# Next quad's input in the first projection's bank, a fourth token buffer, later pack loads and a new order of steps in a conv, attention and Fourier block

## What is computed

```python
for L in (0, 1):                               # conv block
    rw = sigmoid(mean(x, tokens) @ Wr + br)    # router: four weights per image
    h  = relu(bn(x @ mix(rw, Wpw) + rw @ bpw)) # first projection, 24 -> 96
    h  = relu(bn(depthwise3x3(h, mix(rw, Wdw))))
    x  = x + bn(h @ mix(rw, Wpwl) + rw @ bpwl) # second projection, 96 -> 24
t = x.reshape(32, 3136, 24)
y = ln(t); q, k, v = split(y @ Wqkv + bqkv)    # 6 heads of 4
t = t + heads(q @ k.T * 4**-0.5 @ v) @ Wff + bff
t = t + qlinear(relu(qlinear(ln(t), W1, b1)), W2, b2)   # rounded to 5/2-bit float
h = fft(relu(bn(ln(t) @ w1.T)), axis=tokens)
t = t + bn(real(ifft(relu(mixed(h)))) @ w2.T)
t = t + qlinear(relu(qlinear(ln(t), W1, b1)), W2, b2)
```

## Time and profile before

| | us |
|---|---|
| median of 3 runs | 2447.91 |
| lowest and highest | 2443.51, 2450.33 |
| the profiled execution's own time | 2448.76 |
| its span, first to last instruction | 2447.0 |
| PE, DVE, ACT busy | 2087.6, 1924.6, 1583.8 |

### The profile page before, as it was taken

How to read it: one execution, slowest core, us unless ns; L and a number is a source line. 1 busy time by engine, 2 the same in 40 slices (tenths; PEclk the granted TensorE clock), 3 DMA queues, 4 the chain that set the end, 5 groups by cost and what they waited for, 6 DMA issues and landing times.

```text
span 2447.0 us, 48861 instructions
## 1 busy us (share of the span) xinstructions
PE 2087.6 (85%) x19720; PEld 1234.5 (50%) x19720; DVE 1924.6 (79%) x3745; ACT 1583.8 (65%) x2704; POOL 114.6 (5%) x290
## 2 busy tenths in 40 slices
PE   3777988999979989999789987898889998887865
PEld 2233433664446634665347634376347644663753
DVE  4986988799949999699959996698978999366253
ACT  3344447775777677765777666776767667767544
POOL 0000000000000000000000000000000000000000
PEclk9887989999979999999989997899999999987765
DMA  5001000100020000100020002000010000000000
GB/s 147 1 1 21 1 1 5 18 2 1 1 40 2 2 1 15 28 2 1 1 40 2 2 1 41 1 2 1 1 32 2 2 1 1 22 2 1 21 1 20
DMA packets 108591, 29.62 MB, mean 12 GB/s; under 512 B 104144, under 2 KB 104272, under 8 KB 107984
## 3 DMA queue, kind: packets, MB, share of 16 engines
q1 hardware_dynamic: 108368, 26.50, 5.3%
HBM read 16.85 MB, written 9.63 MB: 11 GB/s over the span
## 4 chain that ended last, share of the span: by engine, by line
DVE 40%; PE 36%; ACT 13%; issue 7%; SPq 3%; DMA 1%; ACTq 0%; DVEq 0%
DVE acc L1505 19%; PE P L757 7%; PE P L738 5%; PE P L972 4%; DVE SQ L1670 3%; PE P L1064 3%; SPq L598 3%; DVE arena L1654 3%; PE P L909 2%; DVE arena L1670 2%; PE P L779 2%; DVE roots L1670 2%; PE P L806 2%; PE P L985 2%; DVE T L1521 1%
## 5 line engine op out<-in xcount | busy, mean ns | idle before, releaser
L1505 DVE SCALAR_TENSOR_TENSOR acc<-H,Dm,acc 128x784 f32<-128x784 f32 x1024 | 999.2, 1029 | 30.7 <-ACT acc L1140 30.3
L738 PE MATMUL P<-T,Wk 112*128 112x448 f32 (+1 forms) x768 | 385.7, 593 | 55.7 <-ACT H L1133 32.2
L757 PE MATMUL P<-H,diag 64*64 64x392 f32 x4608 | 404.5, 501 | 15.5 <-DVE T L1521 12.4
L1133 ACT ACTIVATE H<-P,biasA 128x448 f32<-128x448 f32 (+1 forms) x384 | 237.3, 622 | 206.0 <-PE P L738 182.7
L757 PEld LDWEIGHTS P<-H,diag 64*64 64x64 f32 x4608 | 174.9, 135 | 228.7 <-issue 191.1
L738 PEld LDWEIGHTS P<-T,Wk 112*128 112x128 f32 x768 | 130.8, 200 | 172.2 <-ACT H L1133 104.1
L1163 ACT ACTIVATE acc<-P,biasT 128x392 f32<-128x392 f32 x128 | 71.7, 584 | 128.8 <-PE P L757 128.8
L1140 ACT ACTIVATE acc<-H,Dm 128x784 f32<-128x784 f32 x128 | 121.6, 950 | 8.1 <-PE P L779 5.8
L1169 ACT ACTIVATE acc<-acc,biasA 128x784 f32<-128x784 f32 x128 | 118.4, 948 | 10.7 <-DVE acc L1505 10.4
L997 PE MATMUL P<-pack_b,arena 128*96 128x112 f32 x928 | 112.3, 268 | 10.6 <-DVE roots L1670 4.6
L972 PEld LDWEIGHTS P<-pack_b,arena 113*64 113x64 f32 x1792 | 112.7, 216 | 16.8 <-issue 7.6
(11 more groups left out here) (209 smaller groups left out, 3630.0 us busy)
## 6 DMA issues: line engine op xcount, KB each, us to landing
xin<-in_x SPq DMA_DIRECT2D x224, 42.0 KB, 2.3
out_y<-arena SPq DMA_DIRECT2D x8, 1176.0 KB, 6.1
pack_b<-in_pack_b SPq DMA_DIRECT2D x1, 3870.5 KB, 17.5
arena<-in_pack_s SPq DMA_DIRECT2D x1, 1584.0 KB, 8.6
pack_a<-in_pack_a SPq DMA_DIRECT2D x1, 1084.0 KB, 5.3
pack_i<-in_pack_i SPq DMA_DIRECT2D x1, 320.0 KB, 3.2
arena<-in_pack_k SPq DMA_DIRECT2D x1, 192.0 KB, 3.4
```

The source lines that it names most:

```text
L738: pe.matmul(conv_rows(slice(0, 128), HB[(NP * s + e) % len(HB)], n), Wk1[:, 128 * j:128 * (j + 1)], image_rows(T[q % 3], a, n), start=True ...
L757: last = pe.matmul(conv_rows(slice(64 * h, 64 * (h + 1)), CVB + r, HH), diag[64 * r:64 * (r + 1), tap, :], H1[64 * r:64 * (r + 1), slot(s, ...
L1133: act.activation(H1[:, slot(s, j), o:o + n, 1:1 + HW], conv_rows(slice(0, 128), HB[(NP * s + e) % len(HB)], n), ACT.Relu, bias=biasA[:, j, ...
L1505: ins = ve.scalar_tensor_tensor(a, H1[:, slot(s, j), r:r + SR, c:c + HW], Dm[:, j, tap:tap + 1], a, ALU.mult, ALU.add)
```

## The change

Next quad's transposes and the logits use bank 0 alone (quad 0 keeps three banks for its transposes). They wait for the previous quad's first projections to be read (`h1_ready`) in place of its last `cv_added`; the wait for `cv_added` moves to DVE, ahead of the mixing of the weights. The input's row sums have a tensor of their own, `part_in`. A fourth T buffer frees `copy_in` from the output of quad q-3. Packs s and b are loaded after all of quad 0's input. The 36 diagonal matmuls of a strip are three steps of 12 in place of one. POOL waits for its own last memset. All four orders in `TURNS` are new.

```diff
 TURNS = {
     "gpsimd": (
-        "d1 c9 m2 c3 b1 c2 m1 c6 b2 c2 m2 c4 b1 c1 m1 d1 c2 b3 m1 d1 c2 m1 c2 b1 c1 m1 c5 b1 c1 b2 c1 m1 c1 m1 "
+        "c9 m1 d1 m1 b1 c6 m1 c4 b2 c2 m1 c1 m1 c1 b1 c3 d1 m1 b1 c2 b1 c3 b1 m1 c1 m1 c1 b1 c1 m1 b1 c4 b1 c2 "
...
-    XG = 4
+    XG, TB = 4, 4
...
+    def input_banks(q):
+
+        return CB if q == 0 else CB[:1]
...
-        Ts = [sb(f"T{n}", [R, TOK]) for n in range(3)]
+        Ts = [sb(f"T{n}", [R, TOK]) for n in range(TB)]
...
-        part = sb("part", [R, 8])
+        part, part_in = sb("part", [R, 2 * NS]), sb("part_in", [R, NCK])
...
-        LGB, CVB = 2, 1
+        LGB, CVB = 0, 1
...
             load(0, range(XG))
-            for key in ("a", "s", "b"):
+            sp.dma_start(pack_t["a"], packs["a"]).then_inc(par_loaded["a"].sem, 16)
+            load(0, range(XG, NCK))
+            for key in ("s", "b"):
                 sp.dma_start(pack_t[key], packs[key]).then_inc(par_loaded[key].sem, 16)
             for q in range(NQ):
-                load(q, range(XG, NCK))
+                if q > 0:
+                    load(q, range(XG, NCK))
...
                 pool_e.memset(bdw[2][:, 0:MR], 0.0).then_inc(ones_ready.sem, 1)
+                pool_e.wait_ge(ones_ready.sem, ones_ready.at(q, 2))
...
             def input_transposes(q):
+                IB = input_banks(q)
...
                     if g == 0 and not first(q):
-                        pe.wait_ge(cv_added.sem, cv_added.at(q, 0))
-                    if g >= 3:
-                        pe.wait_ge(in_evac.sem, in_evac.at(q, g - 2))
+                        pe.wait_ge(h1_ready.sem, h1_ready.at(q, 0))
+                    if g >= len(IB):
+                        pe.wait_ge(in_evac.sem, in_evac.at(q, g - len(IB) + 1))
                     for s in range(BPG):
                         o = RC * (BPG * (n % XG) + s)
-                        last = pe.transpose(P[0:R, g % 3, BLK * s:BLK * (s + 1)], xin[:, o:o + R], par["ident"][0:BLK, 0:BLK])
+                        last = pe.transpose(P[0:R, IB[g % len(IB)], BLK * s:BLK * (s + 1)], xin[:, o:o + R], par["ident"][0:BLK, 0:BLK])
...
                 for tap in range(NTAP):
                     dy, dx = tap // 3, tap % 3
+                    if tap and dx == 0:
+                        yield
...
             def copy_in(q):
+                IB = input_banks(q)
                 for g in range(NCK):
                     yield
-                    if g == 0 and q >= 3:
-                        act.wait_ge(ot_psum.sem, ot_psum.at(q - 2, 0))
+                    if g == 0 and q >= TB:
+                        act.wait_ge(ot_psum.sem, ot_psum.at(q - TB + 1, 0))
...
-                                   ACT.Copy, accum_out=part[:, g:g + 1]).then_inc(in_evac.sem, 1)
+                                   ACT.Copy, accum_out=part_in[:, g:g + 1]).then_inc(in_evac.sem, 1)
...
-                link(ve.tensor_reduce(pool[:, :], part[:, 0:(NCK if L == 0 else 2 * NS)], AX.X, ALU.add), q, "conv")
+                link(ve.tensor_reduce(pool[:, :], part_in[:, :] if L == 0 else part[:, :], AX.X, ALU.add), q, "conv")
...
                 ve.wait_ge(rw_ready.sem, rw_ready.at(q, L + 1))
+                if L == 0 and not first(q):
+                    ve.wait_ge(cv_added.sem, cv_added.at(q, 0))
...
-    nc = _bacc.Bacc("TRN2", target_bir_lowering=False, num_devices=1, dynamic_dma_scratch_size=4096)
+    nc = _bacc.Bacc("TRN2", target_bir_lowering=False, num_devices=1, dynamic_dma_scratch_size=2048)
```

More of the change, by code:

```diff
@@ L738, in hidden @@
                         pe.matmul(conv_rows(slice(0, 128), HB[(NP * s + e) % len(HB)], n), Wk1[:, 128 * j:128 * (j + 1)],
-                                  image_rows(T[q % 3], a, n), start=True, stop=True).then_inc(h1_psum.sem, 1)
+                                  image_rows(T[q % TB], a, n), start=True, stop=True).then_inc(h1_psum.sem, 1)
             def taps(q, L, s):
@@ L806, in layer_norm @@
                         pe.matmul(P[0:R, cen[c % NC], 0:CK], par["cen"][0:R, :],
-                                  T[q % 3][:, CK * c:CK * (c + 1)], start=True, stop=True).then_inc(norm.cen_psum.sem, 1)
+                                  T[q % TB][:, CK * c:CK * (c + 1)], start=True, stop=True).then_inc(norm.cen_psum.sem, 1)
                     if c >= 1:
@@ L1063, in output_transposes @@
                     for s in range(BPG):
-                        last = pe.matmul(P[0:BLK, FB[g % BN], RC * s:RC * (s + 1)], by_token_block(T[q % 3])[:, BPG * g + s, :],
+                        last = pe.matmul(P[0:BLK, FB[g % BN], RC * s:RC * (s + 1)], by_token_block(T[q % TB])[:, BPG * g + s, :],
                                          par["rest"][0:R, :], start=True, stop=True)
@@ L1108, in copy_in @@
             def copy_in(q):
+                IB = input_banks(q)
                 for g in range(NCK):
                     yield
-                    if g == 0 and q >= 3:
-                        act.wait_ge(ot_psum.sem, ot_psum.at(q - 2, 0))
+                    if g == 0 and q >= TB:
+                        act.wait_ge(ot_psum.sem, ot_psum.at(q - TB + 1, 0))
                     act.wait_ge(in_tp.sem, in_tp.at(q, g + 1))
-                    act.activation(by_token_block(T[q % 3])[:, BPG * g:BPG * (g + 1), :],
-                                   P[0:R, g % 3, 0:CK].rearrange("p (s n) -> p s n", s=BPG),
-                                   ACT.Copy, accum_out=part[:, g:g + 1]).then_inc(in_evac.sem, 1)
+                    act.activation(by_token_block(T[q % TB])[:, BPG * g:BPG * (g + 1), :],
+                                   P[0:R, IB[g % len(IB)], 0:CK].rearrange("p (s n) -> p s n", s=BPG),
+                                   ACT.Copy, accum_out=part_in[:, g:g + 1]).then_inc(in_evac.sem, 1)
             def conv(q, L):
@@ L1177, in layer_norm @@
                     k = i * NCK + c + 1
-                    D = T[q % 3][:, CK * c:CK * (c + 1)]
+                    D = T[q % TB][:, CK * c:CK * (c + 1)]
                     if n == 0:
@@ L1516, in conv_end @@
                             yield
-                            t = image_rows(T[q % 3], SR * s + HH * h, HH)
+                            t = image_rows(T[q % TB], SR * s + HH * h, HH)
                             ve.wait_ge(cv_psum.sem, cv_psum.at(q, 2 * (L * NS + s) + h + 1))
@@ L1548, in layer_norm @@
                         ve.wait_ge(fpads_set.sem, fpads_set.at(q, 1))
-                    ve.tensor_tensor(dst[0:R, CK * c:CK * (c + 1)], T[q % 3][:, CK * c:CK * (c + 1)],
+                    ve.tensor_tensor(dst[0:R, CK * c:CK * (c + 1)], T[q % TB][:, CK * c:CK * (c + 1)],
                                      P[0:R, spread[c % NSP], 0:CK], ALU.mult, saturate=False).then_inc(norm.y_ready.sem, 1)
@@ L1591, in attention @@
                     ve.wait_ge(at_psum.sem, at_psum.at(q, c + 1))
-                    t = T[q % 3][:, CK * c:CK * (c + 1)]
+                    t = T[q % TB][:, CK * c:CK * (c + 1)]
                     ve.scalar_tensor_tensor(t, P[0:R, ab[c], 0:CK], cA[:, :], t,
@@ L1681, in fourier @@
                     yield
-                    t = by_column(T[q % 3])[:, 8 * g:8 * g + 8, :]
+                    t = by_column(T[q % TB])[:, 8 * g:8 * g + 8, :]
                     ve.wait_ge(fo_psum.sem, fo_psum.at(q, g + 1))
```

## The result

The changed kernel takes 2372.49 us (median of 4 runs, 2370.68 to 2374.57), the kernel before 2449.12 in the same comparison (4 runs, 2443.51 to 2453.07). The ratio is 0.9689, 95% interval 0.9668 to 0.9711: 76.6 us less, where I had forecast 49. The profiled execution took 2371.59 us, its span 2369.8.

The account below looks back on a forecast made before the run. The prediction took the seven quad boundaries (274.8 us, DVE idle 160.5) as the bound, with PE next; 11 + 26 + 14 - 8 + 6 = 49 us off 2448.8 gave a median of 2399 us, range 2358 to 2438.

Parts of the forecast that it names:

- the boundary closes: Rival: PE idles no more at the seven quad boundaries, giving 2375, or 2333 by DVE's side; chance 0.17.
- Start, -11: Start of quad 0: groups 4 to 6 load before packs s and b, 13.5 us earlier, 2.3 lost; net -11 us.
- DMA waits, -26: Quad boundaries: PE's 32.6 us of waits for input loads after the start fall to 6, counted as -26 us.
- Transposes moved, -14: Boundaries: 23 of 49 transpose groups move ahead of the last second projection into PE's idle time, 0.6 us each; -14 us.
- The first rival: Only the start gains, as unchanged norm, feed-forward and Fourier steps set the boundary; 2425 to 2440, chance 0.18.
- One bank, +8: Boundary transposes: each group must be copied before the next in the single bank; +8 us, between 0 and 26.
- The rival of a late ACT: ACT copies the one bank late, PE waits 2.3 us for each of 42 groups; +53 us, 2501, chance 0.08.
- Clock, -6: Boundaries to quads 1 and 6: halved gaps let part of PE's work run at the upper clock, 3 us each; -6 us.
- my mixture: Boundary clocks read as mixtures of 1.2 and 2.4 GHz, so halved gaps turn only part of the work warm; 3 us each.
- Taps in three steps: Inside the quads: three steps of 12 diagonal matmuls equal the same 36, other steps between them in 38 strips; priced 0.
- The rest at nothing: Logits in bank 0, the moved cv_added wait, h1_ready wait, POOL's wait and fourth T buffer priced at 0.
- The tail: Stretch after the last tap, 368.6 us, expected to shift but stay within 8 us of that length.

Follow-up runs that it names:

- e3: Kernel before with only the start changed: groups 4 to 6 of quad 0 loaded ahead of packs s and b, setup_rest behind the first block's last tap; 2436.60 us.
- e4: Changed kernel with the 23 early groups of input transposes moved right behind the previous quad's last second projection, still one bank; 2434.14 us.
- e1: Changed kernel's code with the order of steps and loads of the kernel before, except that GpSimd keeps the new order; 2461.52 us.
- e2: e1 with the next quad's 23 early groups of input transposes moved ahead of the last second projection, in bank 0; 2484.81 us.
- e7: Changed kernel with each strip's 36 diagonal matmuls in one piece at the place of the first third, only PE's order differing; 2450.52 us.
- e12: e2 with 60 of 64 strips cut, the two steps behind each block of diagonal matmuls put between its thirds; 2600.89 us.
- e6: e1 with the row-sum tensor widened to 16 columns, so later buffers lie as in the kernel before modulo 64 bytes; 2464.37 us.
- e5: Changed kernel with the row-sum tensor widened to 16 columns, so later buffers lie as in the kernel before modulo 64 bytes; 2367.92 us.
- e8: Changed kernel with the store of quad q-2 placed behind all seven loads of quad q+1; 2376.96 us.
- e11: e1 with 60 of 64 strips cut, the two steps behind each block of diagonal matmuls put between its thirds; 2577.86 us.

## Why the prediction was right, and where it was not

The direction, the place and the range were right; the size was not, by 28 us (77.2 by the spans, where the sum said 49). The 2372.5 us lie below the 2380 to 2425 of the forecast itself, in the band of the rival "the boundary closes" (2333 to 2380, chance 0.17), of which the wide range had taken in half. The number is that rival's, its mechanism is not: PE still idles 39.3 us in the boundaries. By the account of the spans, the forecast's own terms against what was measured are: start 11 and 16.1; idle time of PE in the boundaries 26 - 8 = 18 and 22.5; work of PE there 14 + 6 = 20 and 44.1; nothing and -5.6 for insides and tail. So most of the miss is in the work. By the steps of the prediction:

- **Start, -11.** In the changed kernel -16.1, alone (e3) -8.9. The times of the chain came out: group 4 at 16.94, last copy done at 22.69 (I took 22.2), first tap at 36.7.
- **DMA waits, -26.** 32.6 became 7.5: -25.1. The 7.5 left are where I put 6: 1.1 at quad 3, 2.4 at quad 5, and three groups at quad 6.
- **Transposes moved, -14: this is the step that failed, by what it left out.** The term itself held: by the same windows cut to the transposes, they took 34.03 us of PE in the boundaries before and 19.65 after, 14.4 less. But PE's work there fell by 44.1. The other 29.7 is the work of middle and back, in part run at a better clock and in part moved out: the windows hold 1559 matmul records before and 1308 after, 251 fewer, and only 80 of them are transposes. The rows allow an estimate of the two parts: PE's busy time in each window times its granted clock is the work at full clock, in sum 170.4 us before and 143.7 after. So 26.7 us were moved out where I had 14, and the lower clock cost 42.6 before and 25.1 after. The other moved records are the Fourier output, the transposes of the output, norms and feed-forward. I read the new order for the groups of input, and priced nothing else that it moved, though the same paragraph counted 20 us of idle PE inside the quads to put it in. The first rival rested on the same error: "the same norm, feed-forward and Fourier steps as before" was not so.
- **One bank, +8.** 5.8 us of waits for ACT's copies, in 11 places. e4 shows what it is with 19 groups directly behind another: 30.2 in 27 places. The rival of a late ACT decided from 1.04 us over all 42 groups; e4 has 0.72, the changed kernel 0.14, so even the experiment nearest to it stays under.
- **Clock, -6: the second term that was too small.** By the same estimate it gave 17.5 us, 42.6 less 25.1. Granted 0.67 and 0.72 at quads 1 and 6, where PE still idles 11.6 and 12.2 us, against 0.66 and 0.63 before; 1.00 at quads 4 and 7, where it idles 1.6 and 1.0, against 0.90 and 0.79. The rule of the Trainium skill that I had set against my mixture ("TensorE: Matmul & The Clock Gate", Part 1: an idle array falls to the lower level, a busy one runs at the upper) fits these four rows, and the -12 that I had put down by it was nearer to the 17.5 than my 6. The other rows are mixed: 0.94 at quad 2 with 2.4 us idle, 0.83 at quad 3 with 4.4, and at quad 5 the clock fell, from 0.87 to 0.72, at much the same idle time (6.4 and 6.2 us), which the sums of idle time do not account for. I had also expected over 0.7 in each boundary; quad 1 has 0.67. A closed gap was what I had no row for.
- **Taps in three steps, 0, between -10 and +5.** Mis-sized most of all: undone alone the cut costs 78 or 101 us, and a cut by rule in the old order 116. It has no price of its own. The place of the cuts is part of the order, and the order only fits the insides of the quads with them.
- **The rest at nothing.** The code edits with the old order (and GpSimd's new one) are 0.6% slower (e1); the last section's rows are about as large, which does not show them to be the cause. The tail, +2.5, held.

What the sum had right was by terms that a trace shows as waits. What it missed is what the order moved without a wait being named, and there the experiments say more than any sum: early input alone costs 23 us (e2); the new order without it keeps 12 us in the boundaries and is 62 us slower than with it (e4); and without its cuts it is no faster than before (e7). All together give 77, of which the start alone gives 9 (e3). Which share of the rest belongs to which can't be told, since none of the others stands alone.

## What to carry to other kernels

Where a change brings a new order of steps, read the whole order over the stretch that you price, and count every instruction that leaves it, not only those that the change names. A long run of matmuls is at once an obstacle for short steps that are ready and a cover for those that are not: cut it only where the trace says that the next step's input is there. The tuned order here could not be taken apart or completed by rule: each of the eight edits of this kind (e2, e4, e7 to e12) lost 4 to 116 us against the kernel that it started from. Only e3, which moves loads and constants of the start, gained (8.7 us).

## What the runs showed of the hardware that I had not expected

**Single short DVE instructions that take up to 2.7 us, at fixed places of the program.** The copies that e1 slowed down, min, median and max in ns, of before and then of the changed kernel:

```profile
L564 DVE COPY thirdsm<-mid x112: 180/184/1147, 224.1 to 2199.1; 32x112 bf16<-32x112 bf16 x112
```

```profile
L571 DVE COPY thirdsm<-mid x112: 179/184/2690, 208.3 to 2111.6; 32x112 bf16<-32x112 bf16 x112
```

The median is the same; a few are long. Among the copies, conversions and small scalings of DVE, 7 are over 0.6 us above their own median before (9.2 us in sum), 15 in e1 and in e6 (27), 13 in the changed kernel (21). Counted along DVE's instructions with its waits on semaphores, the copies of e1 that take over 0.7 us are numbers 618, 993, 1443, 2432, 2691 and so on, and those of e6, with all buffers 32 bytes away, are the same numbers. The changed kernel has 614, 972, 1443, 2431, 2697. Before, and in e3, where the same instructions run at other times, they are 617, 1143, 2159, 2685. e4, e5, e7 and e8 have those of the changed kernel. So they belong to places in the stream of instructions, and neither a shift of the buffers by 32 bytes nor another time changes them; the data were the same in all runs. The 18 us more in e1 (16 above the medians) are about what its DVE and its insides have lost (14.7 and 16.6). What happens at those places is not shown here; no run was made for it.

**In e11 the clock stands at half for the 5.9 us behind a wait of 4.19 us.** This is one place. The windows of e11 around the strip above:

```profile
497.20:499.40 2.20, 2.19 (x25) 0.80 (x24) 2.13 (x6) 0.93 (x2) 0.00 (x0) 1.00 0.00 0
503.60:509.50 5.90, 5.90 (x27) 1.75 (x27) 3.11 (x6) 0.44 (x1) 0.00 (x0) 0.50 0.02 4
510.60:512.80 2.20, 2.18 (x25) 0.79 (x24) 0.00 (x0) 0.00 (x0) 0.00 (x0) 1.00 0.00 0
```

The granted clock is 1.00 in the first third, 0.50 in the stretch behind the wait and 1.00 again in the last third. The wait cost 4.19 us and the slower matmuls behind it 2.8 more (4.20 in place of 2.21 for the third, 1.81 in place of 0.98 for the centring).
